# An attention block's second layer: products in column tiles in the transposes' PSUM bank, norm transposes in the products' bank, and the second layer's transposes behind the values

## What is computed

```python
q, k_t, v_t = heads(x @ W_q), heads(text @ W_k), heads(text @ W_v)
probs_t = softmax(einsum('bhsd,bhtd->bhst', q, k_t) * scale)
text_out = einsum('bhst,bhtd->bhsd', probs_t, v_t)
qsem = l2norm(einsum('bhst,bte->bhse', probs_t, text))
fused = q @ k_ip * scale + 0.5 * qsem @ l2norm(ip).T
ip_out = (softmax(fused) * mask) @ v_ip
out = (text_out + ip_out) @ W_out + b_out + x
```

## Time and profile before

| | us |
|---|---|
| median of 3 runs (3484.27 to 3486.09) | 3485.79 |
| the profiled execution | 3485.28 |
| its span | 3483.4 |

### The profile page before, as it was taken

The page is one execution under the profiler, slowest core; times in us unless marked ns, Lnnn a source line. Parts: engine busy times, 40 slices in busy tenths (PEclk is TensorE's granted clock), DMA queues, the critical chain, the costliest instruction groups (busy, mean ns, idle before and its releaser), DMA issues. The chain is left out here.

```text
span 3483.4 us, 96098 instructions
## 1 busy us (share of the span) xinstructions
PE 3335.4 (96%) x34878; PEld 3131.8 (90%) x34878; DVE 2438.3 (70%) x7677; ACT 2314.2 (66%) x6485; POOL 1329.5 (38%) x1657
## 2 busy tenths in 40 slices
PE   5899999999999999999999999999999999999997
PEld 4789999999899999999999899998999999899987
DVE  6657677767767767677767767767677776777655
ACT  4566676766767676676766767676676766767654
POOL 2223343333434433343433434433343333434333
PEclk9999999999999999999999999999999999999998
DMA  6432324223142332324223142332324223142310
GB/s 157 157 116 69 105 63 126 74 86 103 54 123 70 108 90 68 108 63 122 78 83 105 54 123 68 106 94 63 113 64 118 82 82 106 54 124 68 94 51 11
DMA packets 210732, 313.84 MB, mean 90 GB/s; under 512 B 31232, under 2 KB 167520, under 8 KB 210272
## 3 DMA queue, kind: packets, MB, share of 16 engines
q1 hardware_dynamic: 209984, 307.53, 30.5%
q10 hardware_dynamic: 288, 0.16, 0.0%
HBM read 267.97 MB, written 14.42 MB: 81 GB/s over the span
## 5 line engine op out<-in xcount | busy, mean ns | idle before, releaser
L997 ACT ACTIVATE SE<-PS,mx 128x77 f32<-128x77 f32 (+1 forms) x2560 | 674.8, 355 | 271.9 <-DVE mx L1248 271.2
L1461 POOL TENSOR_TENSOR SE<-SE,rs 128x512 f32<-128x512 f32 (+1 forms) x640 | 552.7, 869 | 625.7 <-DVE rs L1270 625.7
L1454 POOL TENSOR_TENSOR n<-qq,p_half 128x4 f32<-128x4 f32 x320 | 327.4, 1023 | 987.0 <-DVE qq L1299 987.0
L1265 DVE TENSOR_REDUCE sums<-SE 128x4 f32<-128x512 f32 (+1 forms) x640 | 368.3, 576 | 217.8 <-ACT SE L997 217.3
L985 ACT ACTIVATE PTs<-PT 128x1024 f32<-128x1024 f32 (+1 forms) x320 | 326.5, 1020 | 242.3 <-PE PT L811 240.7
L933 ACT ACTIVATE qk<-PG 128x512 f32<-128x512 f32 (+1 forms) x640 | 326.3, 510 | 127.2 <-PE PG L612 125.5
L773 PE MATMUL PW<-w_o,OTs 128*128 128x160 f32 x2560 | 408.8, 303 | 0.0
L1248 DVE TENSOR_REDUCE mx<-PS 128x8 f32<-128x1024 f32 (+1 forms) x320 | 323.0, 1010 | 115.6 <-PE PS L793 113.4
L827 PE MATMUL PV<-PTs,v_sb 128*64 128x128 f32 (+1 forms) x5120 | 351.1, 279 | 12.3 <-DVE SE L1291 12.0
L773 PEld LDWEIGHTS PW<-w_o,OTs 128*128 128x128 f32 x2560 | 359.7, 191 | 0.0
L876 PE MATMUL PV<-later 73*128 73x86 f32 x2560 | 331.0, 272 | 2.3 <-ACT later L1006 1.4
(11 more groups left out here) (209 smaller groups left out, 8439.1 us busy)
## 6 DMA issues: line engine op xcount, KB each, us to landing
q_slice<-q_split SPq DMA_DIRECT2D x630, 192.0 KB, 2.4
vc_slice<-vc_split SPq DMA_DIRECT2D x155, 512.0 KB, 4.0
kc_slice<-kc_split SPq DMA_DIRECT2D x150, 256.0 KB, 2.9
q1st<-q_hi SPq DMA_DIRECT2D x320, 32.0 KB, 2.1
k1st<-k_hi SPq DMA_DIRECT2D x160, 38.5 KB, 2.2
xres<-in_x_dram SPq DMA_DIRECT2D x32, 160.0 KB, 2.7
q1st<-q_lo SPq DMA_DIRECT2D x160, 32.0 KB, 2.1
out_dram<-x SPq DMA_DIRECT2D x64, 80.0 KB, 1.6
```

What stands on the lines that cost most here:

```text
L997: last = a_(SE[:, n % 4, J * i:J * i + J], PS[:, e, J * at:J * at + J], ACT.Exp, bias=mx[:, q % 2, 4 * e + at:4 * e + at + 1])
L1265: v.tensor_reduce(sums[:, n % 2, :], SE[:, n % 4, 0:4 * J].rearrange("p (i j) -> p i j", j=J), AX, ALU.add)\
L1454: gp.tensor_tensor(n20[:, b % 2, 4 * w:4 * w + 4], qq[:, b % 2, 4 * w:4 * w + 4], p_half[:, 0:4], ALU.pow)\
L1461: gp.tensor_tensor(e, e, rs[:, n % 2, :].unsqueeze(2).to_broadcast([128, 4, J]), ALU.mult)\
```

## The change

Layer 1's products (`probs_v1`) are computed in two halves of 64 output rows each, so 8 matmuls and not 4, with 64-column weights, in the tiling that `probs_v` has. They go to `PT` bank 0 and stand in slot 0 of the beat after, behind `probs_v`. `unit_out`, which reads them, moves on VectorE to slot 0 behind `softmax_in`; `unit_norms` and GpSimd's `norms_of` move to slot 1. `probs_transposed1` moves behind the values, and ScalarE's `pt1_out` behind its slot's query job. The norm transposes leave the jobs and their two banks; they go to `PV` with a semaphore of their own (`xT_full`). The tail's vector steps come one slot later, its jobs stay. Where layer 1 is alone (`alone`), its products go to `PV` and its scores alternate between `PS` and `PT`.

```diff
-    TAIL_JOB = {"ipT": 7, "ip": 10, "oT1": 13, "y": 16}
+    TAIL_JOB = {"ipT": 6, "ip": 9, "oT1": 12, "y": 15}
...
         def tail_slot(g, b):
-            return 3 * l1_beat(g, W1 * b + W1 - 1) + 7
+            return 3 * l1_beat(g, W1 * b + W1 - 1) + 8
+
+        def alone(g, k):
+            return l1_beat(g, k) > DUOS * GROUPS + 1
+
+        def products1_bank(g, k):
+            return PV if alone(g, k) else PT[:, 0, :]
+
+        def scores1_bank(g, k):
+            return PS[:, 0, :] if alone(g, k) and k % 2 else PT[:, 1, :]
...
-            return first + v, [x for x in late_at(t) if x[0] != "v"]
+            return first + v, [x for x in late_at(t) if x[0] not in ("v", "xT")]
...
+                def norm_transposed(name, multiplied):
+
+                    pe.wait_ge(S["nx_done"], NORM[name[1:]] + 1)
+                    if multiplied:
+                        pe.wait_ge(S["ots_done"], multiplied)
+                    if turned_x[0]:
+                        pe.wait_ge(S["nT_dve"], turned_x[0])
+                    if product1[0]:
+                        pe.wait_ge(S["on_done"], product1[0])
+                    for part in range(2):
+                        for b in range(HB):
+                            last = tr(PV[:, HT * part + 128 * b:HT * part + 128 * b + 128],
+                                      nx[:, b, 128 * part:128 * part + 128], ident[:, :])
+                    last.then_inc(S["xT_full"], 1)
+                    turned_x[0] = NORM[name[1:]] + 1
...
@@ probs_v
-                    if product1[0]:
-                        pe.wait_ge(S["on_done"], product1[0])
+                    if turned_x[0]:
+                        pe.wait_ge(S["nT_dve"], turned_x[0])
...
@@ scores1
-                    if j > 1:
+                    if alone(g, k - 1):
+                        pe.wait_ge(S["exp1_done"], j - 2)
+                        pe.wait_ge(S["exp_done"], NL0 * GROUPS)
+                    elif j > 1:
                         pe.wait_ge(S["exp1_done"], j - 1)
...
@@ probs_transposed1
+                    if product1[0]:
+                        pe.wait_ge(S["on_done"], product1[0])
...
-                def probs_v1(g, k, multiplied):
+                def probs_v1(g, k, turned):
...
-                    if multiplied:
-                        pe.wait_ge(S["ots_done"], multiplied)
+                    if alone(g, k):
+                        pe.wait_ge(S["ots_done"], DUOS * GROUPS)
+                        pe.wait_ge(S["nT_dve"], turned_x[0])
+                    elif turned:
+                        pe.wait_ge(S["pts_done"], turned)
...
-                        last = mm(PV[:, GV * i + off:GV * i + off + GS + D1], PTs1[0:TT, 128 * i:128 * i + 128],
-                                  gv[:, b % 2, 2 * w + i // 2, off:off + GS + D1], start=True, stop=True)
+                        for c in range(2):
+                            last = mm(ps[64 * c:64 * c + 64, GV * i + off:GV * i + off + GS + D1],
+                                      PTs1[0:TT, 128 * i + 64 * c:128 * i + 64 * c + 64],
+                                      gv[:, b % 2, 2 * w + i // 2, off:off + GS + D1], start=True, stop=True)
...
@@ TensorE's loop
                         if duo_at(beat - 1):
                             probs_v(*duo_at(beat - 1))
-                    if part == 1 and l1_at(beat - 1):
-                        probs_transposed1(*l1_at(beat - 1), turned)
+                        if l1_at(beat - 2):
+                            probs_v1(*l1_at(beat - 2), turned)
                     if part == 1 and l1_at(beat):
                         scores1(*l1_at(beat), turned)
                     for name in jobs_at(t)[0]:
                         job(name)
+                    if part == 1 and l1_at(beat - 1):
+                        probs_transposed1(*l1_at(beat - 1), turned)
                     if part == 1 and beat > DUOS * GROUPS and l1_at(beat):
                         keep_busy(6)
-                    if part == 2 and l1_at(beat - 1):
-                        probs_v1(*l1_at(beat - 1), multiplied)
                     for name in late_at(t):
                         if name[0] == "xT":
-                            job(name)
+                            norm_transposed(name, min(max(beat, 0), DUOS * GROUPS))
...
@@ ScalarE's loop
-                    if sub == 1 and l1_at(beat - 1):
-                        pt1_out(*l1_at(beat - 1))
...
+                    if sub == 1 and l1_at(beat - 1):
+                        pt1_out(*l1_at(beat - 1))
                     if sub == 2 and l1_at(beat):
                         exp1(*l1_at(beat))
...
@@ VectorE's loop
                     if sub == 0 and l1_at(beat - 2):
-                        unit_norms(*l1_at(beat - 2))
+                        unit_out(*l1_at(beat - 2))
...
+                    if sub == 1 and l1_at(beat - 2):
+                        unit_norms(*l1_at(beat - 2))
                     if sub == 1 and l1_at(beat):
                         softmax1_in(*l1_at(beat))
...
-                    if sub == 2 and l1_at(beat - 1):
-                        unit_out(*l1_at(beat - 1))
...
@@ GpSimd's loop
-                    if sub == 0 and l1_at(beat - 2):
+                    if sub == 1 and l1_at(beat - 2):
                         norms_of(*l1_at(beat - 2))
```

32 lines of the change are left out of this document (17 added, 15 removed).

## The result

The changed kernel takes 3594.27 us in the median (3593.23 to 3595.33), the kernel before 3485.03 beside it: ratio 1.0314, 95% interval 1.0296 to 1.0332. It is 109 us slower, where 3532 had been forecast and 3568 was the upper end. The sign was right, the size less than half of what came (46 of 109 us).

A forecast was written before the change was run, and what follows sets the result against it. The prediction took TensorE to bound the kernel, with thin cover. Its beat terms summed to +3.4 us per group, +51 over 14.9 groups, and -4 at the end: 3485.3 to 3532 us, 1.3% slower; range 3465 to 3568.

The forecast's parts named there:

- Step 1: Layer 1's products on TensorE: 0.60 us as 16 records instead of 0.85, saving 0.25 per beat if nothing waits.
- Step 2: Order on each engine: first query job 0.60 us later, unit_out ending at 4.2, work in the middle of the beat late.
- Beats 8 to 12: Cross-attention's keys: the second key copy ends 1.0 us later and TensorE waits for it; +2.1 us per group.
- Beats 1, 6, 16: Values read out late on VectorE, so the next user of their bank waits; +1.6 us per group.
- Beat 7: L717's first weights no longer wait for the bank the norm transposes held; the largest gain, -1.0 us per group.
- The softmax beats: Beats 2, 3, 4, 13, 14, 19: GpSimd's L1454 moving back helps, later sums take it back; +0.2 us per group.
- The rest: Beats 0, 15 and 18: no late wait there, so each gains 0.26 us; -0.8 us per group.
- The last 20 stand alone: Last 20 product groups, at the end: a loop sets the pace and has 0.25 us less; -4 us (0 to -15).
- A: Rival: TensorE's saving comes through, VectorE's moved work falling into its idle gaps; 3405 us; chance 0.09.
- B: Rival: the bank freed by the norm transposes helps in the other seven norm beats too; 3471 us; chance 0.11.
- C: Rival: both column tiles run wholly side by side, products take 0.43 us; 3481 us; chance 0.06.
- D: Rival: column tiles don't run side by side, products stay at 0.85 us; 3610 us; chance 0.05.

The follow-up runs named there:

- b_tiles: The kernel before with only its products in pairs of 64-column tiles, same place and still in PV; 3492.69 us, ratio 1.0025.
- y_norms: The changed kernel with unit_norms on VectorE behind the copy of the values, and SE1 in three buffers; 3544.26 us.
- x_swap: The changed kernel with the norm copy (and the squares of the context) ahead of the tail's exponential L1107 on ScalarE; 3571.01 us.
- a_exp1: x_swap with exp1 ahead of pt1_out on ScalarE, and pt1_out behind the norm copy in beats with feed-forward or down jobs; 3584.7 us.
- w_full: y_norms with probs_v and products behind slot 0's jobs, unit_out later, a_exp1's ScalarE order, tail's first vector step later, the earlier kernel's order at the end; 3476.85 us.
- x_alone: The changed kernel, but where layer 1 is alone its transposes no longer wait for unit_out of the products before; 3577.24 us.
- x_normpg: The changed kernel with only the norm transposes back among the jobs in their two banks (PG); 3612.92 us.
- w_pg: w_best with the norm transposes among the jobs again, in PG; 3457.88 us.
- w_best: w_full with the tail's first two vector steps placed around softmax_in instead of ahead of the first row sums; 3438.07 us, ratio 0.9864.
- x_whole: The changed kernel with the products in 4 matmuls of 128 columns again, same place and bank; 3706.3 us.
- y_place: y_norms with the products behind the jobs of slot 0, and unit_out behind the first row sums (beats 8 to 12: behind the second key copy); 3600.55 us.
- a_three: The changed kernel with y_norms, x_swap and x_alone together; 3498.91 us, ratio 1.0043.

## Where the prediction held and where it failed

Of the 62 us between the forecast and the measured time, 41 lie in the end (-4 forecast, +37 measured) and 21 in what stands ahead of it (+51 and +72).

- **Step 1 (products 0.60)** was right: 0.70, less 0.10 that probs_v gains. The measured 0.70 for the products alone lies at the upper bound of 0.69; the sum came out as forecast because the change of tiling went from behind probs_v to behind the products. Its doubt of the page's factor of two was right too (0.43 would have been needed). That a matmul in fp32 makes two records is what the trace shows; that these are two passes is the prediction's reading. What the prediction said in passing, that L827's row "holds a change of tiling", was the more important sentence: b_tiles shows that it decides whether anything is saved.
- **Step 2 (who stands ahead of whom)** was right in time and place: query job +0.61, unit_out's end 4.26, key copy +0.97. Beats 8 to 12: predicted +2.1, measured +2.70 (beat 10 +0.75 for +0.3; y_norms takes half of it away, the rest is open). Beats 1, 6, 16: +1.6, measured +1.37. Beats 5 and 17: +1.3, measured +1.02. Beat 7: -1.0, measured -1.25. y_norms shows the mechanism of the key copies and the values by itself; the prediction's sign in the waits came too: the first matmul and first weight load of a query job (L618) wait 32.8 and 54.1 us for the key copy, before 3.8 and 9.8.
- **The softmax beats** came out near their sum by luck: +0.2 forecast, -0.37 measured, but beat 2 has +0.42 for -0.26, beat 3 -0.61 for +0.05 and beat 19 -0.25 for +0.07. The prediction's balance of GpSimd's earlier and later steps does not hold beat by beat; y_norms shortens beats 3 and 4 by a further 0.37 each, the rest was not taken apart.
- **"The rest. Beats 0, 15 and 18 have no such wait: -0.26 each, -0.8"** was the step that failed in the steady part: +0.49, +0.50 and +0.78 were measured, +1.77 together, 2.6 us a group off, and over the 14.9 groups 38 us. For 0 and 15 the prediction had costed the tail's vector steps, "one slot later", at nothing and named no cover: it never asked what L1107 would stand ahead of on ScalarE (x_swap). For 18 it took pt1_out's lateness only to the norm copy and not on to the table load behind exp1 (a_exp1 and w_full take it back). All other beats sum to +3.5, where +4.2 was predicted, so a part of this miss is hidden by theirs.
- **"The last 20 stand alone ... I take -4"** was the step that failed most: +37. The prediction's loop held transposes, pt1_out, products and unit_out as before; the changed order closes it once a beat, with the transposes waiting for unit_out by an added `wait_ge` that the diff shows, and TensorE, idle more, loses clock. x_alone takes 17 to 20 of the 37 back. It also left out that a norm's transposes now hold PV ahead of the last `probs_v`: x_normpg takes 9 back, and w_pg 9 against w_best. The order of the kernel before at the end leaves 8 to 11 us with the norms in PV (w_full 135.8, w_best 138.8) and 2 with the norms in PG (w_pg 129.5). The two gains were not tried together on the changed kernel, so the split of the 37 is not exact.
- **The rivals.** A fell: VectorE is idle 68 us of a group, and the moved work still made others wait, because of what it stands ahead of. B was right in kind, 20 us and not 61. C and D fell by x_whole. The range was built from the bounds of one term (0.54 to 0.69 for the products) and from the rivals; the beats and the end that were costed at a plain gain had no bound above (the end's was 0), and they are what lay outside.

## What to carry to other kernels

A change that moves steps between engines' rows is priced by what each moved instruction now stands ahead of, for every beat in which it occurs, also those in which the step looks idle: 0.27 us of an exponential that waits cost 23 us, 0.45 us of a reduction 50. Where a table shifts steps by "one slot", list for each engine its new next neighbour. Put small-tile matmuls beside matmuls of the same tiling, or the change of tiling takes what they save; and where a phase of the program runs with other banks, look whether the added waits still guard anything there. A bank that is a gain in the steady part can cost at the end (1.8 us a group gained, 9 us lost at the end).

## What was not expected of the hardware

- A change of tiling cost 0.06 to 0.10 us on TensorE at each side (b_tiles: 0.10 ahead of the products, 0.06 in the projection behind them; y_place, beat 7: 0.34 in all, with two changes more than y_norms).
- A table load is 1.28 us, with no drain to be seen around it, and hides well as long as the last exponential is early.
- When TensorE waits more, it is also slower while it works: in the end of the changed kernel the granted clock had a mean of 0.74 (two levels, 1.2 and 2.4 GHz), in x_alone, with the same work and 18 us less of the L885 waits, 0.84; TensorE's busy time fell from 121.3 to 106.0. The eight kernels that have this wait show 0.72 to 0.80 there, x_alone and a_three 0.84 and 0.85.
- A VectorE instruction took up to four times as long beside some of GpSimd's: in y_norms L1358 took 0.24 us in beat 9, where only L1493 ran beside it, and 0.93 at the end of beat 19, where L1485 did for 0.83.
